# Dense rows turned at the start of their step in three parts, and eight instead of six field pairs spread by TensorE

## The reference, cut to what matters

```python
emb = tables[feat_idx, sparse]                       # 2048 x 26 x 32
linear_out = lin_sparse_w[feat_idx, sparse].sum(-1) + dense @ lin_dense_w
x0 = emb; xk = emb; res = []
for w, bb in ((conv1_w, conv1_b), (conv2_w, conv2_b)):
    hp = einsum('bhd,bmd->bhmd', xk, x0).reshape(-1, h * M, E)
    xn = sigmoid(einsum('oi,bid->bod', w, hp) + bb)
    xk, r = xn[:, :half], xn[:, half:]; res.append(r)
cin_out = concatenate(res, 1).sum(-1) @ cin_w + cin_b
deep_x = concatenate([emb.reshape(-1, M * E), dense], -1)
deep_out = tanh-layers 1024, 512, 256 of deep_x, then @ deep_w + deep_b
return linear_out + cin_out + deep_out + bias
```

## Time and profile before

| | |
|---|---|
| median of three runs | 1764.49 us (1760.94 to 1777.09) |
| profiled execution, device time | 1765.62 us |
| its span, first to last instruction | 1763.8 us |
| mean granted TensorE clock | 0.970 of full |
| from the first K fill of tile 0 to the end of the tiles | 68.67 us to about 1468 us |
| PE, DVE, ACT, POOL busy | 91%, 63%, 40%, 42% |

### The profile page before, as it was taken

The page is one execution under the profiler, slowest core; times in us unless marked ns, Lnnn a source line. Parts: engine busy times, 40 slices in busy tenths (PEclk is TensorE's granted clock), DMA queues, the critical chain, the costliest instruction groups (busy, mean ns, idle before and its releaser), DMA issues.

```text
span 1763.8 us, 23496 instructions
## 1 busy us (share of the span) xinstructions
PE 1603.8 (91%) x6840; PEld 691.1 (39%) x6840; DVE 1103.3 (63%) x992; ACT 702.8 (40%) x981; POOL 748.4 (42%) x631
## 2 busy tenths in 40 slices
PE   0799899989898989798989998989898997999998
PEld 0333333323333333233333333323333333877886
DVE  2277677767676767476767875757676776434432
ACT  1444344334343434343434434334343342445443
POOL 6628273728282826373737372637364111000000
PEclk9899999999999999899999999989999999999999
DMA  4678687968697868587878886867687773233231
GB/s 88 127 181 195 158 192 175 201 151 190 162 188 164 188 160 191 139 180 171 182 165 179 192 190 158 183 154 183 164 184 163 188 185 102 90 97 97 88 101 48
DMA packets 111802, 277.59 MB, mean 157 GB/s; under 512 B 26035, under 2 KB 46803, under 8 KB 111703
## 3 DMA queue, kind: packets, MB, share of 16 engines
q1 hardware_dynamic: 98456, 270.11, 63.4%
q0 software_dynamic: 13312, 7.06, 4.2%
HBM read 270.03 MB, written 7.04 MB: 157 GB/s over the span
## 4 chain that ended last, share of the span: by engine, by line
PE 51%; POOL 26%; issue 11%; DMA 5%; ACT 4%; DVE 2%; POOLq 0%; ACTq 0%; DVEq 0%
POOL emb L438 22%; PE y L631 20%; PE bc L745 15%; PE xn L625 12%; DMA emb<-table,idx_stage 5%; PE bc L611 2%; POOL r L453 2%; PE bc L618 1%; POOL r L456 1%; ACT halves L785 1%; PE bc L594 1%; PE bc L603 1%; DVE xb L549 1%; DVE hp L549 1%; ACT r L807 1%
## 5 line engine op out<-in xcount | busy, mean ns | idle before, releaser
L549 DVE TENSOR_TENSOR hp<-bc,xk 128x1024 f32<-128x1024 f32 x384 | 452.7, 1216 | 426.0 <-PE bc L611 426.0
L438 POOL DMA_INDIRECT emb<-table,idx_stage x416 | 504.8, 1213 | 147.0 <-issue 133.2
L549 DVE TENSOR_TENSOR xb<-xb,xk 128x1024 f32<-128x1024 f32 x448 | 547.3, 1266 | 26.2 <-ACT xk L806 25.5
L625 PE MATMUL xn<-sq,w1s 128*128 128x512 f32 x768 | 392.3, 650 | 78.2 <-ACT r L807 74.9
L631 PE MATMUL y<-xb,w2s 128*64 128x512 f32 x1792 | 432.7, 596 | 0.7 <-ACT r L811 0.4
L631 PE MATMUL y<-hp,w2s 128*64 128x512 f32 x1536 | 382.6, 605 | 0.1
L453 POOL TENSOR_TENSOR r<-r 128x512 f32<-128x512 f32 x96 | 123.6, 1294 | 444.0 <-ACT r L811 320.1
L801 ACT ACTIVATE sq<-bc 128x1024 f32<-128x1024 f32 x192 | 182.9, 1026 | 271.4 <-PE bc L618 265.9
L625 PEld LDWEIGHTS xn<-sq,w1s 128*128 128x128 f32 x768 | 146.6, 205 | 272.6 <-issue 140.9
L805 ACT ACTIVATE xk<-xn,bias 64x512 f32<-64x512 f32 x128 | 87.1, 680 | 325.5 <-PE xn L625 323.3
L631 PEld LDWEIGHTS y<-xb,w2s 128*64 128x64 f32 x1792 | 122.1, 137 | 238.4 <-issue 203.5
(11 more groups left out here) (63 smaller groups left out, 1028.4 us busy)
## 6 DMA issues: line engine op xcount, KB each, us to landing
xb<-x_rows SPq DMA_DIRECT2D x896, 256.0 KB, 4.8
w_raw<-W SPq DMA_DIRECT2D x32, 448.0 KB, 3.3
w_raw<-W SPq DMA_DIRECT2D x16, 512.0 KB, 3.3
emb<-table,idx_stage POOLq DMA_INDIRECT x416
x_rows<-deep_t SPq DMA_DIRECT2D x16, 384.0 KB
w_raw<-W SPq DMA_DIRECT2D x8, 256.0 KB, 2.5
hp<-select SPq DMA_DIRECT2D x2, 512.0 KB, 4.8
x_rows<-deep_t SPq DMA_DIRECT2D x16, 45.0 KB
```

The source lines that it names most:

```text
L438: nc.gpsimd.indirect_dma_start(out=emb[:, m, :], out_offset=None, in_=table, in_offset=bass.IndirectOffsetOnAxis(ap=idx_stage[:, m:m + 1], ...
L549: nc.vector.tensor_tensor(product(n)[:, :], x[:, :], xk[sl % 2][:, :], ALU.mult).then_inc(multiplied, 1)
L625: last = nc.tensor.matmul(xn[:, :], w1s[:, k, :], sq[k][:, cols], start=(k == 0), stop=(k == K1 - 1))
```

## The change

Four things change together.

1. `BY_PE` grows from six to eight pairs, in four fills of two; `BY_DMA` shrinks from seven to five. `ORDER` is a new permutation so that the two pairs of each fill lie in different row groups. `of_last` now has three pairs (10, 11, 12) and a step has twelve fills instead of ten.
2. The dense rows are turned in three parts of 3, 3 and 1 transposes right behind the T fill of step 2, no longer at the step's end, and ACT copies them there. POOL's `free_emb` waits for the third.
3. `make_high` moves in ACT's list from before `read_xn` 0 of step 1 to behind `read_xn` 1 of step 1.
4. POOL's gathers are split 6, 14, 20 instead of 12, 18 (with the last four apart), two sums of `r1` change places with them; SP issues the dump ahead of step 3's spreads and waits for it behind them; K and T fills wait for their slots one by one.

```diff
-ORDER = [3, 10, 0, 7, 4, 1, 8, 11, 2, 9, 5, 12, 6]
-BY_PE = (2, 3, 5, 6, 8, 9)
+ORDER = [4, 11, 5, 0, 7, 12, 1, 8, 2, 9, 3, 10, 6]
+BY_PE = (3, 4, 6, 7, 8, 9, 10, 11)
 STEP_WORK = (
     ("fill", (("K", 0), ("K", 1), ("K", 2))),
-    ("of_last", (9, 10, 11, 12)),
-    ("fill", (("T", 0),)),
+    ("of_last", (10, 11, 12)),
+    ("fill", (("T", 0), ("D", 0), ("D", 1), ("D", 2))),
     ("first", 0),
-    ("fill", (2, 3)),
-    ("of_this", (0, 1)),
+    ("fill", (3, 4)),
+    ("of_this", (0, 1, 2)),
     ("first", 1),
-    ("fill", (5, 6)),
-    ("of_this", (2, 3, 4)),
+    ("fill", (6, 7)),
+    ("of_this", (3, 4)),
     ("fill", (8, 9)),
-    ("of_this", (5, 6, 7, 8)),
+    ("of_this", (5, 6)),
+    ("fill", (10, 11)),
+    ("of_this", (7, 8, 9)),
 )
-DEEP_PARTS = range(0, 4), range(4, KD)
+DEEP_PARTS = range(0, 3), range(3, 6), range(6, KD)
-AHEAD = 12, 18
+AHEAD = 6, 14, 20
...
             def tile(t, is_first, ahead):
                 for sl in range(STEPS):
                     s = t * STEPS + sl
+                    if sl == SL_DEEP + 1 and ahead > 0:
+                        dump(t + 1)
...
                 if ahead > 0:
-                    dump(t + 1)
+                    await_dump(t + 1)
...
-                if ahead > 0:
-                    gather(range(AHEAD[1], M - 4))
                 if not is_first:
                     add_up(t - 1, STEPS - 1, r2, r2_step, y2_read, 1, sum2)
                 if ahead > 0:
-                    gather(range(M - 4, M))
+                    gather(range(AHEAD[2], M))
                 add_up(t, 1, r1, r1_step, xn_read, 2, sum1)
                 if ahead > 0:
                     make_low(t + 1)
+                add_up(t, 2, r1, r1_step, xn_read, 2, sum1)
                 add_up(t, 1, r2, r2_step, y2_read, 1, sum2)
-                add_up(t, 2, r1, r1_step, xn_read, 2, sum1)
+                if ahead > 1:
+                    free_emb(t + 1, filled_by(t, SL_DEEP, ("D", 2), ahead))
+                    gather(range(AHEAD[0]))
                 add_up(t, 3, r1, r1_step, xn_read, 2, sum1)
                 if ahead > 1:
-                    free_emb(t + 1, filled_by(t, SL_DEEP, ("D", 1), ahead))
-                    gather(range(AHEAD[0]))
+                    gather(range(AHEAD[0], AHEAD[1]))
                 add_up(t, 2, r2, r2_step, y2_read, 1, sum2)
                 if ahead > 1:
-                    gather(range(AHEAD[0], AHEAD[1]))
+                    gather(range(AHEAD[1], AHEAD[2]))
...
                             for use in uses:
-                                slot_free(t, sl, use, is_first, ahead)
+                                if is_product(use):
+                                    slot_free(t, sl, use, is_first, ahead)
                             for use in uses:
+                                if not is_product(use):
+                                    slot_free(t, sl, use, is_first, ahead)
                                 fill(t, sl, use, ahead)
...
                                     copy_x0(slot_of(sl, use, ahead), (sl + 2) % STEPS)
-                                    if sl == 1 and ahead > 0:
-                                        make_high(t + 1)
+                                if is_d(use) and use in there:
+                                    act.wait_ge(filled, filled_by(t, sl, use, ahead))
+                                    if use[1] < 2:
+                                        copy_deep(slot_of(sl, use, ahead), t + 1, DEEP_PARTS[use[1]], 0).then_inc(deep_copied, 1)
+                                    else:
+                                        copy_deep_last(slot_of(sl, use, ahead), t + 1, 0)
...
                             read_xn((sl + 1) % 2, (sl + 1) % STEPS, what)
-                    if ("D", 0) in there:
...
+                            if what == 1 and sl == 1 and ahead > 0:
+                                make_high(t + 1)
```

More of the change, by code:

```diff
@@ L81, in step_fills @@
         fills = [use for use in fills if not is_t(use)]
-    if sl == SL_DEEP and ahead > 0:
-        fills = fills + [("D", 0), ("D", 1)]
+    if ahead == 0 or sl != SL_DEEP:
+        fills = [use for use in fills if not is_d(use)]
     return fills
@@ L372, in dump @@
             def dump(t):
-                sp.wait_ge(deep_copied, t * 2 + 2)
+                sp.wait_ge(deep_copied, t * 3 + 3)
                 hold()
@@ L379, in dump, with await_dump @@
                              deep_t[0:LAST_E, KD - 1, cols]).then_inc(dumped, 16)
+            def await_dump(t):
                 sp.wait_ge(dumped, t * (16 * DUMPS) + 16 * DUMPS)
@@ L397, in tile @@
                 if ahead > 0:
-                    dump(t + 1)
+                    await_dump(t + 1)
             dump(0)
+            await_dump(0)
             over_tiles(sp, tile)
@@ L471, in _ @@
             free_emb(0, 3)
-            gather(range(AHEAD[1]))
+            gather(range(AHEAD[2]))
             def tile(t, is_first, ahead):
-                if ahead > 0:
-                    gather(range(AHEAD[1], M - 4))
                 if not is_first:
@@ L649, in slot_free @@
                 else:
-                    pe.wait_ge(deep_copied, t * 2 + (3 + held[1]))
+                    pe.wait_ge(deep_copied, t * 3 + (4 + held[1]))
             def fill(t, sl, use, ahead):
@@ L675, in _ @@
                 if k == 2:
-                    pe.wait_ge(deep_copied, 2)
+                    pe.wait_ge(deep_copied, 3)
                 spread_sum(k, k, x0t[0])
@@ L717, in tile @@
                             contract(n)
[L718 to L721, removed]
             over_tiles(pe, tile)
@@ L820, in _ @@
             act.wait_ge(w1_step, 7)
-            copy_deep(2, 0, range(KD - 1), 0).then_inc(deep_copied, 1)
+            copy_deep(2, 0, range(KD - 1), 0).then_inc(deep_copied, 2)
             copy_deep_last(2, 0, KD - 1)
```

## The result

The changed kernel takes 1685.63 us (median of four runs, 1684.58 to 1686.75), the kernel before 1762.72 in the runs beside it: a ratio of 0.959 with an interval of 0.953 to 0.965, so 4.1% faster. The forecast was 1678 with a range of 1667 to 1702. The profiled execution took 1684.58 us, 81.0 less than the one of before (1765.62); the sum of the prediction gave 87.4 less.

A forecast was written before the change was run, and what follows sets the result against it. PE, busy 91% of the span, was taken as the bound, losing time mainly to ACT's `xn` read. 1765.6 - 72.7 - 25.6 - 14.1 + 32 - 7 = 1678 us, range 1667 to 1702.

The forecast's parts named there:

- The hole and its slow clock: PE's `contract_k` waits once a tile for ACT's `xn` read, then runs slowly: both go, -72.7 and -25.6 us.
- The dense waits: K fills behind the dense transposes wait for ACT's slot copies: these waits go, -14.1 us; the seven transposes stay, 0.98 us.
- The fourth group: One more PE fill of two pairs in each of 64 steps, 0.50 us each: +32 us, bounds +28 and +38.
- The size that would have given 1706: A tiling-mode drain as long as the added fill itself would make its term +60 us and the time 1706.
- The -7 us for `contract_k`: Two contractions before the second `contract_k` take 1.97 us, PE short for ACT's third read; three there return 0.11 x 64.
- Slots at margins of a third of a us: Twelve fills on three slots: DVE's products are done 0.33 to 0.6 us before PE wants the slot, so 0.
- rival (a): Slot hand-over costs 0.3 us more, PE waits at two or three places a step: +13 to +32, 1691 to 1710; chance 0.13.
- DMA: "nothing waits on them, so 0": DMA loses 256 of its 896 spreads; nothing waits on them, so the term is 0.

The follow-up runs named there:

- the first experiment: Kernel before with only `make_high` moved behind both reads of step 1; 1669.15 us, ratio 0.943.
- the second experiment: Kernel before with dense rows turned early in two parts and new POOL and SP lists, six pairs by PE, `make_high` at its old place; 1646.65 us, ratio 0.931.
- the fourth experiment: Changed kernel with one contraction behind each K fill instead of all three behind the three fills; 1728.52 us.

## Why the prediction was right, and where its sum was off

- **The hole and its slow clock, -72.7 and -25.6: right.** Waits and clock say so directly, and the first experiment shows that ACT's order alone is enough (1669 us, dense waits left). The second shows that the early turning alone is enough too. I had treated them as two halves of one cure; they are two cures for the same stall, and in the changed kernel the move of `make_high` is worth nothing that can be told from noise (old place again: +1.7 us). By the starts of the T fills, the fourteen steps with a hole were 98.9 us longer than plain ones; the two terms gave 98.3.
- **The dense waits, -14.1: right** in the changed kernel (1.92 us above a plain step before, 0.99 after), but by two errors that cancel: the transposes cost 0.73 us and not 0.98, and the third part's wait for ACT's copy of T, "at worst 0.2 us a tile" and left out of the sum, took 0.25.
- **The fourth group, +32: right in size.** Measured 34.6 by steps (20.54 against 20.0 of the second experiment). How it is made up I had only guessed at: about 0.22 us of its 0.54 is matmul time, the rest is changing shape, 0.2 on entering and 0.1 at the end of the contractions ahead, as the fourth experiment showed when it added such places without adding work. The Trainium skill (TensorEngine Tiling (Array Packing), Key Properties) says that a change of tiling mode drains TensorE; these rows agree that a change costs time, some 0.3 us, but don't show that it is a drain. The size that would have given 1706, 0.94 us a group, didn't come.
- **The -7 us for `contract_k`: the step that failed.** I read 1.97 us for two contractions as a wait for ACT's third read. In the changed kernel a run of two takes 1.86 with no wait at all; what was above 1.79 was mostly the cost of changing shape, which stays. A row of before at 1.90 left some 0.04 us a step to win. Group and return together were to add 0.39 us a step and added 0.54 (20.00 to 20.54), 9.6 us over 64 steps: 7 of them this term, 2.6 the group. The first fill of pairs begins 1.6 us earlier than before (77.55 for 79.16 us), where more of the start ran at the full clock. That leaves 1.6 of the miss of 6.4 on the other side. It isn't behind the slow `contract_k`, since the steps with a hole give only 0.6 more than the sum. From the last T fill to the end of the tiles the kernel before took 53.97 us and the changed one 54.07, although three fourth groups, 1.6 us, had come in: before, the last contractions of both closing steps kept pace with DVE's products and not their own (twelve matmuls in 3.35 us for 2.75), and they no longer do. These 2.1 us, less 0.6 by which the dense layers took longer, are about the rest.
- **Slots at margins of a third of a us: right on this chip.** One wait of 0.42 us in the whole run. On the slower chip, where hand-overs now and then took a us longer, rival (a)'s waits appeared: `PE bc L618 <- DVE hp L556` 25.6 us in 25 waits in the changed kernel with the old place. The changed kernel itself wasn't run there.
- **DMA: "nothing waits on them, so 0": right for the changed kernel**, and that is why the fourth group is a loss: seven pairs fit (share 0.84), so the two pairs moved to PE bought nothing. I added 32 to the sum and didn't ask what the kernel would be without it. Without the group and without the return, which needed the third contraction, the sum gives 1653; the second experiment measured 1647.

## What to carry to other kernels

Before making the producer of a late input faster, see what is queued behind the wait for it: here two moved lines were worth 5.7%. When the stall is gone and nothing else makes the busiest engine wait, that engine is the bound, and each further part must be priced by it; a part that takes load off an engine with room (DMA at 0.84) and puts it on the full one loses, though the bundle still wins. And place two-input GpSimd work away from VectorE's SBUF products: in idle time of GpSimd it cost 12 to 24 us.

## What the runs showed that I had not expected

- Changing between these matmul shapes costs TensorE about 0.3 us per group: 0.44 us for a lone K fill against 0.22 for each more pair of matmuls in the same group, and 1.00 instead of 0.885 for a lone contraction. At the change the weight load (0.19 us) starts only with the new group.
- GpSimd additions of two SBUF inputs beside five VectorE products from SBUF stretch these from 5.75 to 7.3 us, and are stretched themselves, 2.26 for 1.27 us. With eight pairs, VectorE's products at that time come from PSUM and keep their pace: three in 3.47 us beside the low halves.
- The kernel before took 1769 and 1837 us on two chips. On the second, a product started 1.3 us later after a fill than the rule in the row read, and 23 waits with no releaser seen add up to 58.4 us; that this is all of the 4% isn't shown, since no profile of the kernel before was taken there. The order of two variants can't be read across such chips.
